# Building an adjacency matrix from one-hot outer products: float32 operands, and bfloat16 operands with the weight split in three

## The reference, cut to what matters

```python
def gin_layer(x, src, dst, ew, w1, b1, w2, b2):
    msg = x[src] * ew[:, None]
    agg = jax.ops.segment_sum(msg, dst, num_segments=x.shape[0])
    h = agg + x
    h = jax.nn.relu(h @ w1 + b1)
    return h @ w2 + b2
```

## Time and profile before

| what | value |
|---|---|
| median of three runs | 5283.54 us |
| span of the profiled execution, first to last instruction | 5276.6 us |
| instructions | 62207 |
| PE / PEld busy over the span | 62% / 47% |
| VectorE (DVE) busy | 51% |
| ScalarE (ACT) busy | 11% |
| GpSimd (POOL) busy | 53% |
| mean granted TensorE clock | 0.695 |

### The profile page before, as it was taken

The page is one execution under the profiler, slowest core; times in us unless marked ns, Lnnn a source line. Parts: engine busy times, 40 slices in busy tenths (PEclk is TensorE's granted clock), DMA queues, the critical chain, the costliest instruction groups (busy, mean ns, idle before and its releaser), DMA issues. The chain is left out here.

```text
span 5276.6 us, 62207 instructions
## 1 busy us (share of the span) xinstructions
PE 3273.3 (62%) x12140; PEld 2478.4 (47%) x12140; DVE 2710.8 (51%) x10052; ACT 595.9 (11%) x1968; POOL 2774.9 (53%) x2942
## 2 busy tenths in 40 slices
PE   1999999999826565555556665555666444444443
PEld 1888888865413443443444443333444333333333
DVE  5877778631244555555553555555552433333332
ACT  2111111130012000000003000000003000000001
POOL 2000000001136777777754777777773777777774
PEclk9866655699857777777778777777767555555555
DMA  2011111156404444444442444444441322222222
GB/s 64 33 52 54 56 56 49 51 217 198 192 21 96 108 109 108 108 109 109 108 85 66 108 109 108 109 108 109 108 106 28 57 57 56 56 57 56 56 56 24
DMA packets 246405, 451.23 MB, mean 86 GB/s; under 512 B 163277, under 2 KB 165075, under 8 KB 241470
## 3 DMA queue, kind: packets, MB, share of 16 engines
q0 software_dynamic: 122928, 318.15, 25.5%
q1 hardware_dynamic: 111150, 128.71, 7.3%
q10 hardware_dynamic: 12144, 2.18, 0.2%
HBM read 392.00 MB, written 57.21 MB: 85 GB/s over the span
## 5 line engine op out<-in xcount | busy, mean ns | idle before, releaser
L486 POOL DMA_INDIRECT rows_all<-gat_tab,ell x2664 | 2517.4, 945 | 822.3 <-issue 624.0
L989 PE MATMUL banks<-rows_all,ident 128*128 128x264 f32 (+1 forms) x5328 | 1797.5, 507 | 1560.0 <-PEq L117 1553.2
L989 PEld LDWEIGHTS banks<-rows_all,ident 128*128 128x128 f32 x5328 | 1299.8, 285 | 2057.3 <-issue 1871.6
L1539 DVE COPY lrel<-m_all 128x8 f32 x666 | 132.6, 199 | 1520.7 <-DMA rows_all<-gat_tab,ell 1196.8
L1564 DVE TENSOR_TENSOR rows_all<-rows_all,banks 128x1024 f32<-128x1024 f32 (+1 forms) x666 | 685.0, 1042 | 136.4 <-DVE ex_in L1552 136.4
L848 PE MATMUL banks<-rows_all 128*128 128x52 f32 x3328 | 667.8, 392 | 81.1 <-PEq L117 80.8
L848 PEld LDWEIGHTS banks<-rows_all 128*128 128x128 f32 x3328 | 656.2, 307 | 99.4 <-issue 97.8
L1239 DVE TENSOR_SCALAR rows_all<-lane,src_hi 128x128 f32<-128x128 f32 x1664 | 479.4, 288 | 152.9 <-DVEq L117 151.1
L1240 DVE TENSOR_SCALAR rows_all<-lane,src_lo,src_w 128x52 f32<-128x52 f32 x1664 | 518.2, 311 | 0.0
L779 ACT ACTIVATE banks<-ex_in 128x40 f32<-128x40 f32 x666 | 138.3, 208 | 3075.6 <-ACTq L117 3075.6
L486 POOL DMA_INDIRECT edges<-sw_d,edge_pick x28 | 27.1, 968 | 849.8 <-POOLq L117 837.9
(11 more groups left out here) (268 smaller groups left out, 2016.8 us busy)
## 6 DMA issues: line engine op xcount, KB each, us to landing
rows_all<-gat_tab,ell POOLq DMA_INDIRECT x2664
x_t<-adj_d SPq DMA_DIRECT2D x11, 3328.0 KB, 11.0
y_t<-adj_d SPq DMA_DIRECT2D x11, 3328.0 KB, 10.9
adj_d<-x_t SPq DMA_DIRECT2D x7, 3328.0 KB, 10.5
adj_d<-y_t SPq DMA_DIRECT2D x6, 3328.0 KB, 11.2
ell<-ell_d SPq DMA_DIRECT2D x666, 2.5 KB, 1.8
acc<-key_d SPq DMA_DIRECT2D x1, 1664.0 KB, 6.1
acc<-vec_d SPq DMA_DIRECT2D x1, 1664.0 KB, 18.8
```

The lines of the kernel that those rows point to most:

```text
L486: return g.indirect_dma_start(out=dst, out_offset=None, in_=table, in_offset=bass.IndirectOffsetOnAxis(ap=idx, axis=0))
L989: last = t.matmul(sum_ps[u % SUMS][:, 0:width], ident[:, :], rows[u][:, r * width:(r + 1) * width], start=(r == 0), stop=(r == SLOTS - 1))
```

## The change

The one-hots become bfloat16. The number 1, and the lanes up to 127, are exact in it. The weight isn't, so it is split: the weight rounded to bfloat16, the rest rounded, and the rest of that. The three sum to the float32 weight exactly. For each destination TensorE now runs three bfloat16 matmuls, with the same `hi_hot` as weights and the three parts of the weighted `lo_hot` as moving operands, and PSUM adds them.

VectorE no longer works destination by destination. `one_hot` has five operations for a group of 16: one compares for `lo_hot` (128 x 832), one for `hi_hot` (128 x 2048), and three multiply `lo_hot` by a part of the weight (128 x 832 each). The numbers that belong to a destination are broadcast along the lanes. To keep two neighbouring elements in the innermost dimension, `split_sources` writes each of them twice side by side (`hi_two`, `lo_two`, `w_two`, [P, P, 2] in bfloat16), and the broadcast is over the pairs. So `split_sources` grows from 6 operations to 13. The mark and wait around `low` make the multiplications wait for the `lo_hot` comparison, with the `hi_hot` comparison issued in between. The sizes of the rings, the order of the work, and all other stages are unchanged.

```diff
+WEIGHT_PARTS = 3
-        lane_i, lane = sb("lane_i", [P, P], I32), sb("lane", [P, P])
+        lane_i, lane = sb("lane_i", [P, P], I32), sb("lane", [P, P], BF16)
-        src_hi, src_lo, src_w = ([sb(f"{n}{u}", [P, P]) for u in range(3)] for n in ("src_hi", "src_lo", "src_w"))
+        src_hi, src_lo, src_w = (sb(n, [P, P]) for n in ("src_hi", "src_lo", "src_w"))
+        hi_two, lo_two = ([sb(f"{n}{u}", [P, P, 2], BF16) for u in range(3)] for n in ("hi_two", "lo_two"))
+        w_two = [[sb(f"w_two{u}_{k}", [P, P, 2], BF16) for k in range(WEIGHT_PARTS)] for u in range(3)]
...
                 for q in range(GROUP_DST):
-                    last = t.matmul(part_ps[n][:, q, :], hi_hot[n][:, q, :], lo_hot[n][:, q, :], start=True, stop=True)
+                    for k in range(WEIGHT_PARTS):
+                        last = t.matmul(part_ps[n][:, q, :], hi_hot[n][:, q, :], lo_w[n][k][:, q, :], start=(k == 0), stop=(k == WEIGHT_PARTS - 1))
...
+            def twice(t):
+                return t[:, :].unsqueeze(2).to_broadcast([P, P, 2])
             def split_sources(u):
...
-                link(v.tensor_copy(src_w[u][:, :], w_ps))
+                link(v.tensor_copy(src_w[:, :], w_ps))
                 signal(turned_free)
...
+                link(v.tensor_scalar(src_hi[:, :], src_hi[:, :], ROUND, None, ALU.add))
+                link(v.tensor_copy(w_two[u][0][:, :, :], twice(src_w)))
+                link(v.tensor_scalar(src_hi[:, :], src_hi[:, :], -ROUND, None, ALU.add))
+                link(v.tensor_tensor(src_w[:, :], src_w[:, :], w_two[u][0][:, :, 0], ALU.subtract))
+                v.tensor_copy(hi_two[u][:, :, :], twice(src_hi))
+                link(v.tensor_copy(w_two[u][1][:, :, :], twice(src_w)))
+                link(v.scalar_tensor_tensor(src_lo[:, :], src_hi[:, :], float(-T), src_lo[:, :], ALU.mult, ALU.add))
+                link(v.tensor_tensor(src_w[:, :], src_w[:, :], w_two[u][1][:, :, 0], ALU.subtract))
+                v.tensor_copy(lo_two[u][:, :, :], twice(src_lo))
+                link(v.tensor_copy(w_two[u][2][:, :, :], twice(src_w)))
             def one_hot(u, c):
...
+                def pairs(ap):
+                    return ap.rearrange("p q (h e) -> p q h e", e=2)
+                def lanes(width):
+                    return lane[:, 0:width].rearrange("p (h e) -> p h e", e=2).unsqueeze(1).to_broadcast([P, GROUP_DST, width // 2, 2])
+                def each(two, width):
+                    return two[:, of, :].unsqueeze(2).to_broadcast([P, GROUP_DST, width // 2, 2])
                 take(dve, hot_free[n])
-                for q in range(GROUP_DST):
-                    d = c * GROUP_DST + q
-                    v.tensor_scalar(hi_hot[n][:, q, :], lane[:, :], src_hi[u][:, d:d + 1], None, ALU.is_equal)
-                    last = v.tensor_scalar(lo_hot[n][:, q, :], lane[:, 0:PAIR * T], src_lo[u][:, d:d + 1], src_w[u][:, d:d + 1], ALU.is_equal, ALU.mult)
+                low = link.mark(v.tensor_tensor(pairs(lo_hot[n]), lanes(PAIR * T), each(lo_two[u], PAIR * T), ALU.is_equal))
+                v.tensor_tensor(pairs(hi_hot[n]), lanes(P), each(hi_two[u], P), ALU.is_equal)
+                link.wait(low)
+                for k in range(WEIGHT_PARTS):
+                    last = v.tensor_tensor(pairs(lo_w[n][k]), pairs(lo_hot[n]), each(w_two[u][k], PAIR * T), ALU.mult)
                 last.then_inc(hot_ready[n], 1)
```

More of the change, by code:

```diff
@@ L249, in program @@
         mores_i = sb("mores_i", [P, PAIRS], I32)
-        hi_hot = [rows_all[:, n * GROUP_DST * P:(n + 1) * GROUP_DST * P].rearrange("p (q c) -> p q c", c=P) for n in range(PART_RING)]
-        lo_hot = [rows_all[:, PART_RING * GROUP_DST * P + n * PART_W:PART_RING * GROUP_DST * P + (n + 1) * PART_W]
+        hot_room = rows_all[:, :].bitcast(BF16)
+        hi_hot = [hot_room[:, n * GROUP_DST * P:(n + 1) * GROUP_DST * P].rearrange("p (q c) -> p q c", c=P) for n in range(PART_RING)]
+        lo_room = hot_room[:, PART_RING * GROUP_DST * P:]
+        lo_w = [[lo_room[:, (n * WEIGHT_PARTS + k) * PART_W:(n * WEIGHT_PARTS + k + 1) * PART_W].rearrange("p (q r) -> p q r", r=PAIR * T)
+                 for k in range(WEIGHT_PARTS)] for n in range(PART_RING)]
+        lo_hot = [lo_room[:, (PART_RING * WEIGHT_PARTS + n) * PART_W:(PART_RING * WEIGHT_PARTS + n + 1) * PART_W]
                   .rearrange("p (q r) -> p q r", r=PAIR * T) for n in range(PART_RING)]
@@ L1222, in weigh_edges @@
                 signal(edge_w_ready)
+            def twice(t):
+                return t[:, :].unsqueeze(2).to_broadcast([P, P, 2])
             def split_sources(u):
                 take(dve, edges_turned)
-                v.tensor_scalar(src_hi[u][:, :], src_ps, 1.0 / T, 0.5 / T - 0.5, ALU.mult, ALU.add)
-                v.tensor_scalar(src_lo[u][:, :], src_ps, half_off[:, 0:1], None, ALU.add)
-                link(v.tensor_copy(src_w[u][:, :], w_ps))
+                v.tensor_scalar(src_hi[:, :], src_ps, 1.0 / T, 0.5 / T - 0.5, ALU.mult, ALU.add)
+                v.tensor_scalar(src_lo[:, :], src_ps, half_off[:, 0:1], None, ALU.add)
+                link(v.tensor_copy(src_w[:, :], w_ps))
@@ L1229, in split_sources @@
                 signal(turned_free)
-                link(v.tensor_scalar(src_hi[u][:, :], src_hi[u][:, :], ROUND, None, ALU.add))
-                link(v.tensor_scalar(src_hi[u][:, :], src_hi[u][:, :], -ROUND, None, ALU.add))
-                link(v.scalar_tensor_tensor(src_lo[u][:, :], src_hi[u][:, :], float(-T), src_lo[u][:, :], ALU.mult, ALU.add))
+                link(v.tensor_scalar(src_hi[:, :], src_hi[:, :], ROUND, None, ALU.add))
+                link(v.tensor_copy(w_two[u][0][:, :, :], twice(src_w)))
@@ L1234, in one_hot @@
+                v.tensor_copy(lo_two[u][:, :, :], twice(src_lo))
+                link(v.tensor_copy(w_two[u][2][:, :, :], twice(src_w)))
             def one_hot(u, c):
                 n = c % PART_RING
-                take(dve, hot_free[n])
-                for q in range(GROUP_DST):
-                    d = c * GROUP_DST + q
-                    v.tensor_scalar(hi_hot[n][:, q, :], lane[:, :], src_hi[u][:, d:d + 1], None, ALU.is_equal)
-                    last = v.tensor_scalar(lo_hot[n][:, q, :], lane[:, 0:PAIR * T], src_lo[u][:, d:d + 1], src_w[u][:, d:d + 1], ALU.is_equal, ALU.mult)
+                of = slice(c * GROUP_DST, (c + 1) * GROUP_DST)
```

## The result

The changed kernel takes 4917.83 us (median of 4 runs, 4916.65 to 4919.42) against 5283.07 us before: a ratio of 0.9309, 95% interval 0.9296 to 0.9323. 365 us are gone. The spans of the profiled executions differ by 359, 5276.6 and 4917.9. The changed kernel's execution took 4919.42 us, 1.5 more than its span; before's must then have been the fastest of its runs (5278.24 us), so most of the 6.9 us that I had put around its span is the difference between runs.

The account below looks back on a forecast made before the run. The bound was VectorE's one-hots plus a stall set by the aggregation, TensorE close behind. Pairs falling from 72.6 to 52.0 us save 226.6, the first stretch 30.9, the last 17.3: 274.8 in all, hence 5008.7 us; range 4935 to 5165.

Parts of the forecast that it names:

- VectorE's ring: Build, each pair: VectorE's work of 35.4 us plus a stall of 13.95 us set by the aggregation, 49.35 us.
- TensorE's sum: Build, each pair: TensorE's groups, aggregation and small matmuls, 65.2 us before the change and 48.0 us after.
- VectorE's operations: One-hot groups and `split_sources` on VectorE: 3.25 us a group in place of 6.6, and 4.2 us for `split_sources`.
- Rival A: VectorE's one-hots: two-element steps with a broadcast operand cost more than dense ones, 4.6 us a group, 5100 us; chance 0.10.
- rival B: VectorE's one-hots: operations run at one element a cycle, 6.0 us a group, 5212 us; chance 0.08.
- TensorE's price: One-hot matmuls on TensorE: 94 ns a record at 1.2 GHz (49 at 2.4), 4.5 us a group (2.35).
- lower bound: One-hot matmuls on TensorE: weight load vanishes, 52 columns in one pass cost 43 ns, 2.1 us a group; 4944 us.
- Rival C: One-hot matmuls on TensorE: weight loads cost by record, not byte, 217 ns each, 10.4 us a group, 5507 us; chance 0.05.
- The aggregation: TensorE's block in each pair: stays at 14.2 us; up to 9 us a pair more if longer at 1.2 GHz.
- The head of a pair: VectorE at the start of each pair: 3.9 us, of which 2.8 is issue, carried over unchanged.
- The rub: Build, each pair: two sums so near each other add 2.65 us, where 1.5 us were over before.
- The edges: Edge gathers, needed after two groups, now 7.7 us in place of 14: costed at nothing, 12 us for every us late.

Follow-up runs that it names:

- e1_no_pairs: Changed kernel with each broadcast operand repeating one element, without the pair of equal neighbours innermost; 5106.8 us against 4917.8 for the changed kernel.
- e8_batch_f32: Kernel before with only the batching: float32 one-hots, three VectorE operations a group in place of 32; 5196.8 us against 5283 for the kernel before.
- e4_narrow: Changed kernel with the second and third matmul of each destination cut from 52 to 16 columns; 4903.8 us against 4917.8 for the changed kernel.
- r3_no_jumps_pe: Changed kernel with TensorE's pair loop written out and its branch for large nodes taken out, a repeat; 5604.0 us against 5628.8 for `r1_after`.
- r1_after: The changed kernel unaltered, measured again where the kernel before takes 5994 us; 5628.8 us.
- e3_six_matmuls: Changed kernel with six matmuls for a destination in place of three, VectorE's work the same; 4961.7 us against 4917.8 for the changed kernel.
- e7_spread_unrolled: Changed kernel with the aggregation in four pieces and the pair loops written out on TensorE and VectorE; 5544.4 us where the kernel before takes 6015.
- e5_spread: Changed kernel with the aggregation cut in four pieces ahead of groups 2 to 5; 5579.8 us where the kernel before takes 6015.

## Why the prediction was right or wrong

- **The bound** was right: VectorE's ring, its work plus the stall in the aggregation. After the result was known, the same sum gave 59 us for `e1_no_pairs` (58.8 measured), and TensorE's sum gave 65.2 us for the case in which it is the bound (66.0 in `e8_batch_f32`).
- **VectorE's operations** were right. A group takes 3.15 us (3.25 said), `split_sources` 3.9 (357.50 to 361.43 us; 4.2 said). Rival A and rival B are out. The page of the Trainium skill that spoke against the change (Vector Engine (DVE) Microarchitecture Reference, section 5.2), whose rows are for sources that hop, isn't borne out for this pattern: runs of one 4-byte word, read again and again, go at full rate, 1219 ns for 2048 elements.
- **TensorE's price** was the step that failed: "I take 94 ns (49), 4.5 us (2.35), near the upper bound, since the load was the limit". Measured 44.3 and 27 ns. The load was the limit in float32, and from that I concluded that it would stay the limit; `e4_narrow` shows that a bfloat16 load of 128 columns hides below 52 columns and takes no more than 29 ns, where I had put the float32 record's at 204. At 1.2 GHz the lower bound in the text (43 ns) was the value. The Trainium skill's fast path was cited beside the sum, and I gave it no weight in the forecast. In the stall of before's form, 4.5 + 14.2 + 2.35 - 7.1, this is 2.36 + 1.05 = 3.4 us a pair, some 40 us in all, the largest single term of the miss. It isn't all of it: with the lower bound the prediction's own sum gave 4944 us, 26 more than measured. Rival C is out by the same number.
- **The aggregation** was carried over at 14.2 us; it takes 12.5 in the mean of the first six (12.0 from 379.04 to 391.06, 13.6 where the clock rises late), 1.7 us a pair. The 14.2 was one pair's; the mean of the kernel before is 14.0. The forecast asked only whether its clock could get worse. In the kernel before its first records, 0.43 us apart, ran at 1.2 GHz, behind float32 one-hots at the same clock; behind the bfloat16 ones it is at 2.4 GHz from its start in some pairs (granted clock 1.00 from 379.74 to 391.06 us) and rises later in others (mean 0.89 from 247.00 to 259.70).
- **The head of a pair**, 3.9 us before and carried over, fell to 1.8: issue time of 33.4 us in the build became 7.4. 2.1 us a pair, 25 in all. It is 7.4 with one matmul as with three, 29.7 with the aggregation in pieces, 14.0 with the loops written out as well, and none in `e1_no_pairs` and `e8_batch_f32`, where VectorE's operations are up to 2.3 us long. These numbers fit a cover like TensorE's: at the end of a pair the sequencer loads a register and branches, and this shows only if the operations queued ahead run out. In the kernel before these are 0.2 us each, and with the pieces there is a wait for TensorE right ahead of it. No run tests this by itself, so it stays open.
- **The rub** of two equal sums, 2.65 us, didn't come: with TensorE's sum at some 30 us, only the short waits of 0.9 us are over the ring. 1.7 us a pair.
- **What I had not seen** works the other way: TensorE's branches. They stood in the trace of before as rows of the sequencer, 3.7 us a pair and 5.0 more in every second one, hidden behind a backlog. "Costed at nothing" should have named them with their cover. They put a wait of 3.6 to 4.6 us on every second pair, 1.9 on the mean; taking them out gave 1.4 a pair (`r3_no_jumps_pe` against `r1_after`). That the time came out no lower still is this term working against the others: without it the miss would have been some 15 to 20 us larger, so part of the closeness is luck.
- Sum of a pair: 35.4 to 32.3 of work (head 2.1, groups 0.8, the rest 0.2), stall 13.95 to 9.6 (price -3.4, aggregation -1.7, 0.7 that I can't place), branches 0 to 1.9, rub 2.65 to 0.9: 52.0 to 44.7. Times 11 that is 80 us, with 6.7 at the first and 2.3 at the last stretch 89 of the 91 us that were missed.
- **The edges** did come late, as feared, by next to nothing: 1.7 us in three waits.
- **The range** was too narrow below. Its lower end, 4940, varied only the operand prices and kept the head, the aggregation and the rub of before. All three turned out smaller.

## What to carry to other kernels

When two engines feed each other through a small ring, add up the ring: the work of one engine plus the stall that the other's longest block sets. It told the outcome of undoing one side (`e1_no_pairs`) to 1%. What to do next stands in the same sum: cut the block in pieces between the others. When everything around gets shorter, look through the trace for what passed beside the old backlog, here the sequencer's branches: it may surface next. And look at the pairs one by one before taking their mean: the kernel before already alternated. An end of a range that varies only the changed operations is no end: what was carried over unchanged moves too.

## What the runs showed of the hardware

- A two-input VectorE operation on bfloat16 runs at twice the float32 rate if each operand has two neighbours innermost, also if the pair is broadcast (1219 ns for 2048 elements), and at the float32 rate if a broadcast element has step 0 innermost (2285 ns, the float32 time of 2284 in `e8_batch_f32`).
- A bfloat16 matmul with its load of 128 weight columns costs 44.3 ns at 1.2 GHz with 52 columns, 29 with 16, and 27 at 2.4 GHz with either; the float32 record with 52 columns 217 and 114.
- In `e8_batch_f32` five groups of float32 one-hots ran back to back for 34.6 us, and the granted clock stayed at 0.50 (1.2 GHz); in `e3_six_matmuls` it rose to 1.00 (2.4 GHz) within 6.6 us of bfloat16 groups back to back. Windows of PE, the first three of `e8_batch_f32`:

```profile
354.00:364.00 10.00, 10.00 (x49) 0.50 0.00 0
364.00:374.00 10.00, 10.00 (x48) 0.50 0.07 16
374.00:384.00 10.00, 10.00 (x48) 0.50 0.01 2
```

- A branch past the matmuls of eight further groups costs TensorE's sequencer 3.5 to 4.3 us, the loop's branch back over two pairs 4.8. It was hidden where the queue held matmuls. VectorE's operations started 1.2 to 1.5 us late behind its register load and branch, and 4.0 to 5.0 behind the end of its loop, where nothing covered them (`e7_spread_unrolled`, `e5_spread`, the kernel before).
